# A two-layer attention network on one core: value products moved forward, weight splitting moved to GpSimd, the first spread in another bank, and maxima turned in 64-row tiles

## The reference

```python
# layer 0, D = 8, text = ctx[:, :77], ip = ctx[:, 77:]
q = _split_heads(hidden_states @ Wq.T, H)
out_text = _merge_heads(_attend(q, _split_heads(text @ Wk.T, H), _split_heads(text @ Wv.T, H), sm_scale))
out_ip = _merge_heads(_attend(q, _split_heads(ip @ Wk_ip.T, H), _split_heads(ip @ Wv_ip.T, H), sm_scale))
x = (out_text + out_ip) @ Wo.T + bo + residual
# layer 1
n = _layer_norm(x, ln1_g, ln1_b); x = x + _attention(n, n, a1_wq, a1_wk, a1_wv, a1_wo, a1_bo)
n = _layer_norm(x, ln2_g, ln2_b); x = x + _attention(n, context, a2_wq, a2_wk, a2_wv, a2_wo, a2_bo)
n = _layer_norm(x, ln3_g, ln3_b); x = x + _geglu_ff(n, ff_w1, ff_b1, ff_w2, ff_b2)
```

## Time and profile before

| | |
|---|---|
| Three runs, us | 1616.55, 1592.74, 1612.28 (median 1612.28) |
| Profiled execution, us | 1618.48, its span 1616.7 |
| Mean granted TensorE clock | 0.959 |
| Busy over the span | PE 96%, PEld 75%, DVE 68%, ACT 48%, POOL 26% |

### The profile page before, as it was taken

One profiled execution on the slowest core, in us unless ns is written; L12 is line 12 of the kernel. 1 busy time (PEld: TensorE's weight loads), 2 busy tenths in 40 slices (PEclk: granted clock), 3 DMA queues, 4 the chain that ended last, 5 costly groups with the idle time before them and its releaser, 6 DMA issues.

```text
span 1616.7 us, 40554 instructions
## 1 busy us (share of the span) xinstructions
PE 1544.4 (96%) x17808; PEld 1206.9 (75%) x17808; DVE 1106.0 (68%) x1531; ACT 776.6 (48%) x1062; POOL 419.1 (26%) x375
## 2 busy tenths in 40 slices
PE   7999999998999999999999999999999999999988
PEld 5666656654788888788777877878887887877788
DVE  6777777655677777667567667676667667676666
ACT  4665656555445544556335444444444444443433
POOL 3333323320123222334312212221122222121300
PEclk7999989658999999999999999999999999999999
DMA  5322241100000020000201010101000020000000
GB/s 154 90 58 57 58 153 41 41 3 2 22 2 2 2 92 2 6 2 2 53 22 28 2 28 2 28 2 28 2 1 28 2 70 2 2 2 1 2 13 20
DMA packets 27211, 45.50 MB, mean 28 GB/s; under 512 B 7393, under 2 KB 15521, under 8 KB 26657
## 3 DMA queue, kind: packets, MB, share of 16 engines
q1 hardware_dynamic: 27040, 42.96, 9.1%
HBM read 29.51 MB, written 1.31 MB: 19 GB/s over the span
## 4 chain that ended last, share of the span: by engine, by line
PE 73%; DVE 9%; issue 6%; ACT 5%; POOL 3%; SPq 2%; DMA 1%; POOLq 0%; ACTq 0%; DVEq 0%
PE a_pj L994 7%; PE a_pj L982 6%; PE l_px L1593 5%; PE a_pj L514 4%; PE a_pv L1016 4%; PE a_px L1016 4%; PE l_pscore L1511 3%; PE a_px L555 3%; PE a_pv L541 3%; PE a_px L1031 2%; PE a_pscore L926 2%; PE a_pj L523 2%; PE l_pst L1526 2%; PE a_pst L947 2%; PE a_px L541 2%
## 5 line engine op out<-in xcount | busy, mean ns | idle before, releaser
L1251 POOL TENSOR_TENSOR a_key_sum<-a_probs 128x512 f32<-128x512 f32 x120 | 160.0, 1338 | 469.9 <-ACT a_probs L1084 469.9
L1163 DVE TENSOR_REDUCE a_negmax<-a_pscore 128x2 f32<-128x1024 f32 x160 | 195.7, 1223 | 105.6 <-PE a_pscore L926 105.4
L1084 ACT ACTIVATE a_probs<-a_pst 128x1024 f32<-128x1024 f32 x160 | 164.0, 1025 | 168.3 <-PE a_pst L953 167.7
L1820 DVE TENSOR_REDUCE l_negmax<-l_pscore 128x2 f32<-128x154 f32 x320 | 204.0, 685 | 57.9 <-PE l_pscore L1511 57.0
L1705 ACT ACTIVATE l_probs<-l_pst 128x1024 f32<-128x1024 f32 x160 | 163.9, 1024 | 112.1 <-PE l_pst L1526 111.6
L767 POOL TENSOR_TENSOR a_key_sum<-a_probs 128x1024 f32<-128x1024 f32 x40 | 96.0, 2401 | 243.3 <-ACT a_probs L601 243.3
L686 DVE TENSOR_REDUCE a_negmax<-a_pscore 128x4 f32<-128x1024 f32 x80 | 97.7, 1221 | 50.8 <-PE a_pscore L472 50.8
L994 PE MATMUL a_pj<-a_wv_hi,a_ct 128*128 128x256 f32 x640 | 111.1, 285 | 0.8
L1593 PE MATMUL l_px<-l_probs,l_v 128*32 128x256 f32 x1280 | 101.0, 440 | 4.9 <-DVE l_ot L1840 4.8
L1188 DVE RECIPROCAL a_recip<-a_pv 128x256 f32<-128x256 f32 x40 | 70.2, 1756 | 45.4 <-PE a_pv L1022 45.4
L601 ACT ACTIVATE a_probs<-a_pst 128x1024 f32<-128x1024 f32 x80 | 81.9, 1023 | 39.8 <-PE a_pst L498 37.7
(11 more groups left out here) (236 smaller groups left out, 3664.9 us busy)
## 6 DMA issues: line engine op xcount, KB each, us to landing
l_ct<-in_ctx_t SPq DMA_DIRECT2D x8, 512.0 KB, 3.8
l_k_stack<-l_k_hi SPq DMA_DIRECT2D x64, 64.0 KB, 2.1
a_ct<-in_ctx_t SPq DMA_DIRECT2D x8, 512.0 KB, 5.0
a_ct<-in_ctx_t SPq DMA_DIRECT2D x16, 256.0 KB, 5.6
l_q_stack<-l_q_hi SPq DMA_DIRECT2D x80, 32.0 KB, 1.9
a_raw_wv<-in_a_wv SPq DMA_DIRECT2D x2, 1280.0 KB, 10.3
l_x<-in_x_t SPq DMA_DIRECT2D x8, 256.0 KB, 3.8
l_k_stack<-l_k_lo SPq DMA_DIRECT2D x32, 64.0 KB, 2.1
```

The costliest lines, as they stand in the source:

```text
L1084: nc.scalar.activation(probs[:, 2 * i:2 * i + 2, 2 * n:2 * n + 2, :], pst[:].rearrange("p h (k q) -> p h k q", k=2), ACT.Exp, scale=SCALE) ...
L1163: nc.vector.tensor_reduce(to, pscore[:], AX.X, ALU.max, negate=True).then_inc(max_done, 1)
L1251: nc.gpsimd.tensor_tensor(key_sums[n][:, two], probs[:, two, 2 * n, :], probs[:, two, 2 * n + 1, :], ALU.add).then_inc(half_summed, 1)
L1820: last = nc.vector.tensor_reduce(to[:, :, k], pscores[s % 2][:, :, keys], AX.X, ALU.max, negate=True)
```

## The change

- **Value products.** `EARLY` replaces `FIRST_PLAN`. Of sequence 0 only q, ip, text, rest and v0 are projected ahead; v1, v2, v3 come in step 0. Of sequence 1, ip comes at (0, 2), text at (1, 0), v0, v1, v2 in step 1 and v3 at (2, 0), these four in px; q and rest follow at (2, 1) and (2, 3).
- **The first spread.** s0 is made by `project` in pj, at the same place (u = 4, s = 3). s1 and s2 stay in px.
- **low_rest.** Its subtraction goes from DVE to POOL (`split_rest`, behind `split_inputs`); the marks of the second value buffer go from ahead of step 0 to (3, 1).
- **Weights of a1.** `OPEN = S0 - 16`. POOL does both halves of the split of wq (k = 1, 3) and wk (k = 6, 8) and the low half of wv (k = 12 to 14); ACT only copies the high half of wv, in six pieces (k = 11 to 13). The layer norm's bias and low part go from DVE to POOL. wq and wk are loaded after step 24, wv after step 31.
- **Turning in a1.** The 128x128 transpose becomes two of 64 rows each, one per half, in two banks; `place_max` reads both. a2 keeps its own.
- `AT`, the table of memory places, is new throughout.

```diff
-    FIRST_PLAN = {0: ("ip", "text"), 1: (None, None), 2: ("q", "rest"), 3: ("v0", "v1"), 4: ("v2", "v3")}
-    PLAN = {0: ("ip", "text"), 1: ("q", "rest"), 2: (None, "v0"), 3: ("v1", "v2"), 4: ("v3", None)}
+    EARLY = {(0, 0): ("v1", 0), (0, 1): ("v2", 0), (0, 2): ("ip", 1), (0, 3): ("v3", 0),
+             (1, 0): ("text", 1), (1, 1): ("v0", 1), (1, 2): ("v1", 1), (1, 3): ("v2", 1),
+             (2, 0): ("v3", 1), (2, 1): ("q", 1), (2, 3): ("rest", 1)}
+    PLAN = {(0, 1): "ip", (0, 3): "text", (1, 1): "q", (1, 3): "rest", (2, 3): "v0", (3, 1): "v1", (3, 3): "v2",
+            (4, 1): "v3"}
...
+        if (u, s) == (4, 3) and 0 <= b - 1 < B - 1:
+            return ("s0", b - 1)
...
+            if what == "s0":
+                pe.wait_ge(recip_done, m + 1)
+                if m == 0:
+                    pe.wait_ge(small_in, 48)
+                spread_recip(0, pj).then_inc(pj_ready, 1)
+                return
...
-            if s == 1 and t % GROUPS == GROUPS - 1 and t // GROUPS + 2 < B:
-                low_rest(t // GROUPS + 2)
...
+        def split_rest(m):
+            pool.wait_ge(in_ready, m)
+            lo = nts[m % 2][2 * REST:EXT, 2]
+            subtract(lo, x32[2 * REST:EXT, 1], lo.bitcast(FP32)).then_inc(rest_ready, 1)
+            pool.wait_ge(rest_ready, m)
...
             for qt in range(QT):
-                last = nc.tensor.transpose(pscore[:, 0, qt * P:(qt + 1) * P], negmax[:, e % 2, qt, :], ident)
+                for h in range(2):
+                    last = nc.tensor.transpose(pscore[:, h, qt * D1:(qt + 1) * D1], negmax[OWN[h], e % 2, qt, :],
+                                               ident[OWN[h], OWN[h]])
...
-            copy(neg_t[:, e % 2, :], pscore[:, 0, 0:SQ]).then_inc(max_placed, 1)
+            copy(neg_t[:, e % 2, :].rearrange("p (t h q) -> p h t q", t=QT, h=2),
+                 pscore[:, :, 0:P].rearrange("p h (t q) -> p h t q", t=QT)).then_inc(max_placed, 1)
...
+            def high(w, at):
+                pool.wait_ge(loaded[at], 32)
+                nc.gpsimd.tensor_copy(w.hi[:], w.raw[:])
+                nc.gpsimd.tensor_copy(w.rest[:], w.raw_rest[:]).then_inc(w_hi, 1)
+                pool.wait_ge(w_hi, at + 1)
...
+            for at, (w, done, first) in enumerate(((wq, wq_done, 1), (wk, wk_done, 6))):
+                if k == first:
+                    high(w, at)
+                if k == first + 2:
+                    for s in range(2):
+                        low(w, s).then_inc(done, 1)
+                    low_rows(w, done)
+            if k == 4:
                 ln.pool_setup(pool)
                 ln.pool_rstd(pool, 0)
...
-        OPEN, LOAD, FF_OPEN = S0 - 10, 24, S2 - 5
+        OPEN, FF_OPEN = S0 - 16, S2 - 5
```

266 lines of the change are left out of this document (139 added, 127 removed), and 49 rows, old and new, of the table AT.

## The result

Over 20 executions the changed kernel took 1598.75 us in the median (1583.52 to 1616.76), the kernel before 1610.91 (1592.74 to 1628.07); the ratio is 0.994, with a 95% interval of 0.9915 to 0.9967. That is 0.6% less: within 2%, and 36 us above the 1563 us that I forecast, outside the range. Medians and extremes are over all executions; the ratios leave out those more than 1.5% above the fastest of their kernel, so they need not agree with the medians. The profiled execution took 1602.1 us, its span is 1600.3 against 1616.7.

The account below looks back on a forecast made before the run. PE, busy 96% of the span, was taken as the bound, through waits, low-clock stretches and its own work. Terms 5 + 15 - 1 + 26.7 + 10 = 55.7 off 1618.5 gave 1563 us, range 1543 to 1593.

Parts of the forecast that it names:

- the sum: All priced gains and costs added: 55.7 us off the profiled 1618.5 us, 10 of them from a1's turning.
- Start, +5 us: Layer 0's first steps: moved products fill waits for DVE, group 5 at 64.6 us against 70.09; gain 5 us.
- The first score can start when the value product of 18.18 us did: Start of layer 0: first score then or somewhat later, first maxima turned near 27 us.
- steps whose values were made early are shorter still: Start of layer 0: reason given for the start's upper bound, a gain of 8 us.
- The lower bound, 0: Start of layer 0: no gain at worst, since at the low clock the moved work is a wash.
- End of a sequence, +15: Layer 0's sequence ends: DVE earlier and px free, 200.0 us from group 5 to 30 against 215.3; gain 15 us.
- POOL's added work, -1: Step 30: wq's subtractions delay the split of sequence 7, PE waits about 1.2 us once; cost 1 us.
- Steps 31 to 36, +26.7: End of layer 0: no ACT wait for wq or wk, full clock, 49.2 us against 75.9; gain 26.7 us.
- Turning, +10: Half transposes in a1 save tiling changes: 0.25 us less in each of 40 steps, 10 us.
- the rule on transposes and the clock: Skill's rule that transposes do not count as work for the clock gate; the clock would then fall in a1.
- the first rival: Layer 0: the clock still falls for long, one stretch gives back 24 us, 1587 us; chance 0.25.
- the second (POOL is waited for): Layer 0: POOL's work costs twice its price, a1 starts some 6 us late, 1593 us; chance 0.1.

Follow-up runs that it names:

- e4: The changed kernel with the first five steps as before the change: 1587.09 us, ratio 0.988 to the kernel before.
- e3: The changed kernel with ACT's wait for the last stacks moved to step 37 and wq's and wk's low parts one step earlier: 1595.86 us, ratio 0.990.
- e5: The changed kernel with the old start, ACT's stack wait moved to step 37, and wq's and wk's low parts one step earlier: 1562.44 us, ratio 0.970.
- f1: The changed kernel with the waits of steps 30 and 35 repaired and the new start kept, same kernel as e3, another session: 1582.43 us, ratio 0.977.
- f4: The changed kernel with the waits of steps 30 and 35 repaired and the old start, same kernel as e5, another session: 1566.39 us, ratio 0.977.
- e1: The changed kernel with ACT's wait for the last sequence's stacks moved from step 35 to step 37: 1580.66 us, ratio 0.985.
- e7: The kernel before with only the sequence-end edits, first spread in pj and the 32-row subtraction on POOL: 1590.88 us, ratio 0.986.

## Why the prediction failed, point by point

By the turned maxima, the changed kernel's profile is 9.9 us ahead of the one before at group 36 (351.43 against 361.29), where the sum had 45.7. Up to group 5 it lost 7.5 us where I had a gain of 5; from 5 to 30 it gained 8.8 where I had 14; from 30 to 36 it gained 8.6 where I had 26.7. So three terms failed: the start, POOL's wait with the clock behind it, and the wait of ACT that the steps 31 to 36 were said not to have.

- **Start, +5 us: wrong in sign, its size open.** By the ratios it costs 9 us (e4) or 32 (e3 against e5), and nothing in f1 against f4, whose medians differ by 16; the mean of group 10 differs by 14. Two steps of the argument failed. "The first score can start when the value product of 18.18 us did": it can't, for it waits for the first stack's rounding by DVE, which came at 18.56 to 19.54 us in the new starts; the products that I moved away had filled exactly that time. The first maxima were turned at 29.9 to 35.1 us in these profiles, where I had 27. And "steps whose values were made early are shorter still" was put among the upper bounds, where the row of 1.21 us, which I used for the last steps, says what a step without products does: PE waits for ACT, as it then did in steps 3 and 4. The lower bound, 0, was no bound. That these waits are what brings the low clock is argued and not shown, since in e1 the same order took 38.94 us for the first five groups.
- **End of a sequence, +15: right in place and about right in size.** Groups 5 to 30 took 199.99 us in e5 against 200.0, so near only since two errors cancel; alone it gives 22 us (e7), of which some fell to the stretches behind.
- **POOL's added work, -1: place and price right, consequence short.** The wait was 1.3 to 1.8 us, against 1.2. The sum put the clock behind it at nothing; it cost 10 us more in the changed kernel's profile, and nothing or 2 us in the seven others. The copies of wq (1.26 us and 0.72) and the 32-row subtractions (1.58 each) were near my prices, and a1 was not held up.
- **Steps 31 to 36, +26.7: the mechanism was right, a wait was overlooked.** "ACT has nothing of wq and wk to do or to wait for any more" is true, and I stopped there; wv is the third matrix. Its copies moved from step 36 to step 35, ahead of them stood the wait for SP's last transfer, and PE lost 6.7 us and the clock. Gained were 8.6 us in the profile (75.9 to 67.3); with that wait moved, and step 30's gone, 28.3 (47.65 us). Step 35 alone takes 11 to 17 us.
- **Turning, +10: 7.7 us by the steps, mis-sized.** The price in a step was right (0.24 for 0.25), the number of steps was not: 32, not 40. The parts of the price were wrong as well: the first group of L537 still takes 0.32 us where I had 0.23, and the four transposes 0.14 where I had 0.2. So the time behind the turning did not go, and the transposes themselves got cheaper. One reading was off too: from L546's start to L563's the rows have 0.54 us, not 0.57. The Trainium skill, TensorEngine Tiling (Array Packing), Key Properties, says that a change of tiling mode drains the engine; that a drain was saved behind the turning is not what these rows show. Of the rule on transposes and the clock that stood beside the first rival nothing was seen: with four of them in each step PEclk is 1.00 from 410 to 600 us. A short fall in a1 there is, behind the wait of 1.82 us, with the old turning and the new, and the trace of the kernel before has it too (PEclk 0.66 from 655 to 660 us), which the prediction overlooked.
- **The sum**: the profiles of the changed kernel and of e5 have the maxima of group 39 at 373.45 and 336.15 us, 37.3 apart. Of this 8.1 lie ahead of group 10 (the start), 12.2 in groups 28 to 31 and 17.0 in groups 33 to 36, and nothing elsewhere. So the three places hold all of the difference to e5; between the medians, 1598.75 and 1562.44, it is 36.3 us, as much as the forecast was off. How much each takes in a usual execution is known less well, since the start and step 30 vary from one to the next. The rivals that came true are the second (POOL is waited for), at its place but smaller, and the first (the clock falls for long), set off by a wait that I had not expected.

e5 is faster than both kernels: 3% below the one before.

## To carry to other kernels

When work moves to an earlier step, list every wait that stands ahead of it in its engine's program, for the other engines' progress at the new time, and not only the work's own inputs; here one wait for the last of a queue's transfers cost 15 us, and it could stand two steps later at no cost. Where an engine stands still before a first result that comes from elsewhere, whatever fills that time is free, and taking it out gains nothing. And look at one stretch in several executions before pricing it: a wait of 1.3 to 1.8 us cost 1.3 to 3.4 us in seven profiles and 12 in one. Where the time of a kernel comes in clusters, look in a trace of the slower cluster for the place before naming it.
